# Gathering rows of x itself for the first 7.5 of 49 iterations, with the normalised copy of x made in 14 chunks beside them

## The reference

```python
def _layernorm(x, axis=-1, eps=1e-05):
    m = jnp.mean(x, axis=axis, keepdims=True)
    v = jnp.var(x, axis=axis, keepdims=True)
    return (x - m) / jnp.sqrt(v + eps)
...
        def _gcn_layer(x, W, b, edge_weight, edge_src, edge_dst):
            support = x @ W
            msgs = support[edge_src] * edge_weight[:, None]
            agg = jax.ops.segment_sum(msgs, edge_dst, num_segments=N_NODES)
            return agg + b
        h = jax.nn.elu(_gcn_layer(x, W1, b1, edge_weight, edge_src, edge_dst))
        h = jax.nn.elu(_gcn_layer(h, W2, b2, edge_weight, edge_src, edge_dst))
        return h
...
    x = x + _L0_gnn_ref(_layernorm(x, axis=-1), L0_gnn_W1, L0_gnn_b1, L0_gnn_W2, L0_gnn_b2, edge_weight, src, dst)
    x = x + _L0_ffn_ref(_layernorm(x, axis=-1)[None], L0_ffn_W1, L0_ffn_b1, L0_ffn_Wg, L0_ffn_bg, L0_ffn_Wd, L0_ffn_bd)[0]
```

## Time and profile before

| | us |
|---|---|
| median of three runs | 4646.21 |
| the profiled execution | 4650.56 |
| its span, from first to last instruction | 4648.6 |
| first gather of layer one begins | 87.92 |
| last gather of layer one begins | 2057.25 |
| first gather of layer two begins | 2075.61 |
| busy: TensorE, VectorE, ScalarE, GpSimd | 3573.3, 1952.0, 1053.3, 3235.2 |

### The profile page before, as it was taken

One profiled execution on the slowest core, in us unless ns is written; L12 is line 12 of the kernel. 1 busy time (PEld: TensorE's weight loads), 2 busy tenths in 40 slices (PEclk: granted clock), 3 DMA queues, 4 the chain that ended last, 5 costly groups with the idle time before them and its releaser, 6 DMA issues.

```text
span 4648.6 us, 84335 instructions
## 1 busy us (share of the span) xinstructions
PE 3573.3 (77%) x21450; PEld 3350.1 (72%) x21451; DVE 1952.0 (42%) x6618; ACT 1053.3 (23%) x1720; POOL 3235.2 (70%) x3389
## 2 busy tenths in 40 slices
PE   2776766767767767768888888878788888869998
PEld 1666666666666666658888877878787887758887
DVE  8433333333333333334554454444444444463333
ACT  4100000000000000004333333333333333241111
POOL 5777777777777777767777777777777777604444
PEclk6766666666566666668988888898988888789999
DMA  8333333333333333334544444444444444435554
GB/s 281 113 113 111 113 112 112 112 111 112 112 112 111 112 112 112 113 96 122 148 146 143 145 142 146 143 146 140 146 144 145 146 142 145 122 129 175 179 178 148
DMA packets 248132, 626.46 MB, mean 135 GB/s; under 512 B 63398, under 2 KB 110459, under 8 KB 247491
## 3 DMA queue, kind: packets, MB, share of 16 engines
q0 software_dynamic: 170688, 492.87, 37.2%
q1 hardware_dynamic: 76930, 129.30, 7.8%
HBM read 519.25 MB, written 103.63 MB: 134 GB/s over the span
## 4 chain that ended last, share of the span: by engine, by line
POOL 56%; issue 19%; PE 17%; DMA 4%; DVE 2%; POOLq 1%; ACT 1%; DVEq 0%; SPq 0%; ACTq 0%
POOL rows L542 56%; PE pA L1325 8%; PE pA L1193 4%; DMA rows<-xn_scratch,idx 2%; DMA rows<-h_scratch,idx 1%; PE pB L1234 1%; PE pC L1315 1%; PE pB L1315 1%; PE pC L1216 1%; POOLq L328 1%; PE pT L1303 1%; DMA xn_scratch<-rows 0%; DMA rows<-in_x_dram 0%; DVE stats L754 0%; ACT aggT L696 0%
## 5 line engine op out<-in xcount | busy, mean ns | idle before, releaser
L1193 PE MATMUL pA<-S,rows 128*128 128x96 f32 x12544 | 2140.2, 344 | 957.7 <-DMA rows<-xn_scratch,idx 524.4
L1193 PEld LDWEIGHTS pA<-S,rows 128*128 128x128 f32 x12544 | 2020.3, 254 | 1087.7 <-DMA rows<-xn_scratch,idx 400.5
L542 POOL DMA_INDIRECT rows<-h_scratch,idx x1568 | 1496.0, 954 | 495.0 <-issue 486.2
L542 POOL DMA_INDIRECT rows<-xn_scratch,idx x1568 | 1492.7, 952 | 484.3 <-issue 479.1
L866 DVE TENSOR_SCALAR S<-iota_p,tdst,twgt 128x96 f32<-128x96 f32 x3168 | 875.7, 349 | 9.2 <-issue 8.9
L915 DVE TENSOR_TENSOR aggT<-aggT,pA 128x192 f32 x784 | 274.2, 350 | 1252.6 <-PE pA L1193 1116.0
L924 DVE TENSOR_TENSOR zb<-pZ,brow 128x256 f32<-128x256 f32 x198 | 84.1, 425 | 860.8 <-issue 625.7
L625 ACT ACTIVATE stage<-aggT 128x256 f32 x196 | 81.7, 417 | 1390.2 <-DVE aggT L915 1372.6
L1234 PE MATMUL pB<-work,w 128*128 128x128 f32 x3232 | 386.6, 278 | 0.0
L1325 PE MATMUL pA<-aggT,work 128*128 x1680 | 382.0, 381 | 0.0
L1234 PEld LDWEIGHTS pB<-work,w 128*128 128x128 f32 x3232 | 370.1, 192 | 0.0
(11 more groups left out here) (178 smaller groups left out, 2226.5 us busy)
## 6 DMA issues: line engine op xcount, KB each, us to landing
pay_scratch<-work SPq DMA_DIRECT2D x98, 512.0 KB
rows<-xn_scratch,idx POOLq DMA_INDIRECT x1568, 2.8
rows<-h_scratch,idx POOLq DMA_INDIRECT x1568
h_scratch<-work SPq DMA_DIRECT2D x98, 128.0 KB
pay_scratch<-work SPq DMA_DIRECT2D x98, 128.0 KB
work<-in_x_dram SPq DMA_DIRECT2D x97, 128.0 KB
rows<-in_x_dram SPq DMA_DIRECT2D x24, 512.0 KB, 5.7
xn_scratch<-rows SPq DMA_DIRECT2D x24, 512.0 KB, 6.3
```

The costliest lines, as they stand in the source:

```text
L542: pool.indirect_dma_start(rows[:, s, t, :], None, source, bass.IndirectOffsetOnAxis(at, 0))\
L1193: last = mm(to[:, k * W:(k + 1) * W], rows[:, slot, t, k * P:(k + 1) * P], Sx[:, t, :], start=(t == 0), stop=(t == T - 1))
```

## The change

- The stage-1 pass over x is gone. The sync queue loads only the tables, `src` and `dst` first. VectorE clears one half of `aggT` at the very start, ScalarE the other half behind its table copies; `tsrc` is transposed first, and `stage_idx`, which makes the gathers' indices, stands right behind it.
- Of layer one the halves 0 to 14 gather from `x` itself; the halves from 15 on gather from `xn_d`, and the first of these waits until all 14 chunks of `xn_d` are stored.
- The rows of the halves 0 to 14 are normalised in their slots: `row_statistics` and `row_scales` on VectorE and `row_root` and `row_normalise` on ScalarE, for two groups (a pair) at a time, one half ahead of the half whose products are added. TensorE waits for them (`s_na`) instead of the gathers.
- In each of the halves 0 to 13 one chunk of 896 rows of x is loaded, normalised and stored, with ScalarE's own DMA queue; the functions are `chunk_statistics`, `chunk_scales`, `chunk_root`, `chunk_normalise`, `chunk_store`, `load_chunk`.
- The small tiles for statistics lie in the space of `LG`, the chunks in `work`; both are used for something else only in layer two.

The core of the diff (the lines with # name the engine):

```diff
+    LNT = 7
+    LNR = LNT * P
+    LNC = NB // LNT
+    RAWI = LNC // 2
...
# sync queue
-                             frm[0:BODY * GE].rearrange("(c p e) -> p c e", p=P, e=GE)).then_inc(s_rows, 16)
-                sp.dma_start(to[0:FULL_ROWS - BODY, GCH - 1, :],
-                             frm[BODY * GE:FULL_ROWS * GE].rearrange("(p e) -> p e", e=GE)).then_inc(s_rows, 16)
-                sp.dma_start(to[FULL_ROWS - BODY:FULL_ROWS - BODY + 1, GCH - 1, 0:LAST_EDGES],
-                             frm[FULL_ROWS * GE:E].rearrange("(a e) -> a e", a=1)).then_inc(s_rows, 16)
-            for c in range(4, XAHEAD):
-                sp.dma_start(rows[:, c, :, :], x_chunk(c)).then_inc(s_xin[c], 16)
-            for i in runs(sp, LNI):
...
# GpSimd
+                for par in range(2):
+                    iteration(0, x, 2 * q + par, par)
+            iteration(0, x, RAWI - 1, (RAWI - 1) % 2)
+            gathers(0, x, RAWI, RAWI % 2, 0)
+            pool.wait_ge(s_xst, 16 * LNC + 1)
+            gathers(0, xn_d, RAWI, RAWI % 2, 1)
+            with pool.Fori((RAWI + 1) // 2, ITERS // 2) as q:
+                for par in range(2):
+                    iteration(0, xn_d, 2 * q + par, par)
+            iteration(0, xn_d, ITERS - 1, (ITERS - 1) % 2)
...
# ScalarE
+            def load_chunk(c, buf):
+                act.dma_start(xc[buf], x[chunk_rows(c), :].rearrange("(p t) f -> p t f", t=LNT)).then_inc(s_xin, 16)
+
+            def row_root(pair, s):
+                act.wait_ge(s_var, pair + 1)
+                act.activation(std[:, s:s + 2, :], mv[:, s:s + 2, :, 1], ACT.Sqrt, bias=epsc[:, :]).then_inc(s_std, 1)
+
+            def row_normalise(pair, s):
+                act.wait_ge(s_nmr, pair + 1)
+                for n in range(2):
+                    for t in range(T):
+                        last = act.activation(rows[:, s + n, t, :], rows[:, s + n, t, :], ACT.Identity,
+                                              bias=nmr[:, s + n, t:t + 1], scale=rstd[:, s + n, t:t + 1])
+                    last.then_inc(s_na, 1)
+
...
+                act.wait_ge(s_xnmr, c + 1)
+                for t in range(LNT):
+                    last = act.activation(xc[buf][:, t, :], xc[buf][:, t, :], ACT.Identity,
+                                          bias=xnmr[:, t:t + 1], scale=xrstd[:, t:t + 1])
+                last.then_inc(s_xna, 1)
+
+            def chunk_store(c, buf):
+                hold(act, s_xna, c + 1)
+                hold(act, s_xst, 16 * c + 1)
+                act.dma_start(xn_d[chunk_rows(c), :].rearrange("(p t) f -> p t f", t=LNT), xc[buf])\
+                   .then_inc(s_xst, 16)
...
+            load_chunk(0, 0)
+            act.sem_inc(s_xst, 1)
+            for pair in range(HALF // 2):
+                row_root(pair, 2 * pair)
...
+            with act.Fori(0, RAWI) as i:
+                for half in range(2):
+                    h = 2 * i + half
+                    _, start, end = half_flags(act, h)
+                    ticks(act, start, end, lambda j: tick1(j, h))
+                    ahead = (1 - half) * HALF
+                    row_root(2 * h + 2, ahead)
+                    row_normalise(2 * h + 2, ahead)
+                    chunk_root(h)
+                    row_root(2 * h + 3, ahead + 2)
+                    row_normalise(2 * h + 3, ahead + 2)
+                    chunk_normalise(h, half)
+                    chunk_store(h, half)
+                    load_chunk(h + 1, 1 - half)
+
+            act.wait_ge(s_xin, 16 * (LNC + 1))
             act.preload_act_table(ACT.Exp)
...
# VectorE
+                to = idx[:, bass.ds(at, 1), :, :].rearrange("p a g t -> p (a g) t")
+                v.tensor_copy(to, tsrc[:, :, bass.ds(h * HALF, HALF)].rearrange("p t g -> p g t"))\
+                 .then_inc(s_idx[layer], 1)
...
+                    tc.then(v.tensor_reduce(LO[0:n, c], rdst[0:n, c, :], axis=AX.X, op=ALU.min))
+                dve.wait_ge(s_tcopied, GCH)
+                dve.wait_ge(s_tbl_clear, 3)
+                for at in range(AHEAD):
+                    stage_idx(0, at, at)
                 for c in range(GCH):
                     n = P if c < GCH - 1 else TAILG
                     v.tensor_scalar(rrel[0:n, c, :], rdst[0:n, c, :], LO[0:n, c:c + 1], None, ALU.subtract)\
...
+            tables()
+            dve.wait_ge(s_const, 4)
+            v.tensor_copy(identg[:, :, 0:P], ident[:, :].unsqueeze(1).to_broadcast([P, KH, P])).then_inc(s_const, 1)
...
+            def row_statistics(pair, s, value):
+
+                for n in range(2):
+                    dve.wait_ge(s_gath[0][s + n], value)
+                    for t in range(T):
+                        last = v.bn_stats(stats[:, s + n, t, :], rows[:, s + n, t, :])
+                last.then_inc(s_st, 1)
+                hold(dve, s_st, pair + 1)
+                for n in range(2):
+                    for t in range(T):
+                        last = v.bn_aggr(mv[:, s + n, t, :], stats[:, s + n, t, :])
+                last.then_inc(s_var, 1)
+
...
+
+                dve.wait_ge(s_std, pair + 1)
+                v.reciprocal(rstd[:, s:s + 2, :], std[:, s:s + 2, :]).then_inc(s_rstd, 1)
+                dve.wait_ge(s_rstd, pair + 1)
+                v.scalar_tensor_tensor(out=nmr[:, s:s + 2, :], in0=mv[:, s:s + 2, :, 0], scalar=-1.0,
+                                       in1=rstd[:, s:s + 2, :], op0=ALU.mult, op1=ALU.mult).then_inc(s_nmr, 1)
...
+            def chunk_statistics(c, buf):
+
+                dve.wait_ge(s_xin, 16 * (c + 1))
...
+                if layer == 0:
+                    for pair in range(HALF // 2):
+                        row_statistics(pair, 2 * pair, 16 * T)
+                    for pair in range(HALF // 2):
+                        row_scales(pair, 2 * pair)
+                    with dve.Fori(0, RAWI) as i:
+                        for half in range(2):
+                            h = 2 * i + half
+                            ahead, value = (1 - half) * HALF, (i + half + 1) * (16 * T)
+                            ovf, start, end = half_flags(dve, h)
+                            with dve.If(ovf > 0):
+                                wide_groups(0, h)
+                            row_statistics(2 * h + 2, ahead, value)
+                            ticks(dve, start, end, tick1)
+                            edges_pair(0, h, 0)
+                            row_scales(2 * h + 2, ahead)
+                            chunk_statistics(h, half)
+                            row_statistics(2 * h + 3, ahead + 2, value)
+                            edges_pair(0, h, 2)
+                            chunk_scales(h)
+                            row_scales(2 * h + 3, ahead + 2)
+                            stage_idx(0, h + AHEAD, (i & 1) * 2 + half)
+                with dve.Fori(0 if layer else RAWI, ITERS) as i:
                     for half in range(2):
                         h = 2 * i + half
...
# TensorE
+            def rows_ready(layer, i, h, u, half, raw):
+
+                if raw:
+                    pe.wait_ge(s_na, HALF * h + u + 1)
+                else:
+                    pe.wait_ge(s_gath[layer][half * HALF + u], 16 * T * (i + 1))
+
...
+            with pe.Fori(0, RAWI) as i:
+                for half in range(2):
+                    half_of(0, i, half, True, tick1)
+            pe.wait_ge(s_na, HALF * (LNC + 1))
+            for layer, tick in ((0, tick1), (1, tick2)):
```

More of the change, by code:

```diff
@@ L236, in bass_gnn_then_routed_ffn @@
         s_rows_clear = sem("edge_rows_padded")
[L237 removed]
+        s_rows = [sem(f"edge_rows_loaded_{n}") for n in ("src", "dst", "weight")]
         s_w = sem("weights_loaded")
@@ new lines, in gathers @@
+            def gathers(layer, source, i, par, half):
+                for u in range(HALF):
+                    s = half * HALF + u
+                    if u == 0:
+                        hold(pool, s_idx[layer], 2 * i + half + 1)
+                    hold(pool, s_mm[layer], SLOTS * i + s + 1)
+                    for t in range(T):
+                        at = idx[:, 2 * par + half, u, t:t + 1]
+                        pool.indirect_dma_start(rows[:, s, t, :], None, source,
+                                                bass.IndirectOffsetOnAxis(at, 0))\
+                            .then_inc(s_gath[layer][s], 16)
@@ new lines, in iteration @@
+            def iteration(layer, source, i, par):
+                for half in range(2):
+                    gathers(layer, source, i, par, half)
+            with pool.Fori(0, RAWI // 2) as q:
+                for par in range(2):
[7 more added lines that the diff above has]
+                    iteration(0, xn_d, 2 * q + par, par)
@@ L769, in _ @@
-            for i in runs(dve, LNI):
-                if isinstance(i, int) and i == 1:
-                    tables()
-                first_chunk = isinstance(i, int) and i == 0
-                lnc.base, lnc.n = 0 if first_chunk else 2 * SLOTS * i - 1, 0
-                for s in range(SLOTS):
```

(19 more changed lines are left out.)

322 lines of the change are left out of this document (138 added, 184 removed).

## The result

| | before | after |
|---|---|---|
| median, us | 4645.78 (4644.03 to 4648.02, 6 runs) | 4730.0 (4727.4 to 4733.65, 6 runs) |
| ratio | | 1.0181, 95% interval 1.0168 to 1.0194 |
| profiled execution, its span | 4650.56, 4648.6 | 4729.28, 4727.6 |
| first gather of layer one | 87.92 | 23.88 |
| first gather of half 15 | 390.60 | 476.62 |

The change makes the kernel 84 us slower, 1.8%. The first four experiments were timed where the kernel before took 4656.69 us; all later ones where it took about 5700 us, so each ratio is against the kernel before in its own session. Bare times are therefore 11 us too long in the first four when they are set beside 4730, and of the later ones the text uses ratios and traces rather than times.

What follows compares the result with a forecast made beforehand. GpSimd's gathers, 20.1 us a half, were taken to bound layer one. Half 15 would begin at 476.5 instead of 389.3 us, 87 later: 4738 us profiled, 4733 against the median, which lies 4.4 lower; range 4650 to 4790.

Steps and rivals of the forecast that it cites:

- the ring: In halves 1 to 13 ScalarE (12.9 us) and VectorE (15.4) wait for each other in turn: period 28.3 us.
- Start: Layer one's gathers begin near 18.3 us, 69.6 us earlier, after VectorE's clearing, the casts and the transposes.
- D(0): Moment when VectorE has made the last scales of half 0: 75 us, bounds 68 and 82.
- ScalarE's gap: In each half, ScalarE's completion, waits and two DMA issues 1.0 us, register load and branches 1.4.
- ScalarE's jump back: ScalarE's loop jump in every second half: 0 to 4.1 us for each of six, 12 us taken in all.
- The second tick: Two halves have two ticks; the second waits for TensorE's product, then stage, zneg, zexp: 2.9 us each, 5.8 together.
- 13 turns: From half 0's last scales to half 13's: 13 x 28.3 + 5.8 + 12 us, ending at 460.7.
- The hand-over: Half 15's gathers wait for the last chunk's normalisation, issue and store (7.0), and GpSimd 0.3: 15.8 us.
- The shift: Half 15's first gather moves from 389.3 to 476.5 us, 87 later; nothing differs from there, so the total moves alike.
- Table switches: ScalarE's two tables alternate each half; load taken as 1.28 us without drain; by the skill page 18 us more, 4751.
- first two rivals: GpSimd still paces layer one, 4601 us, chance 0.07; VectorE paces and ScalarE is never late, 4633 or 4659 us, chance 0.11.
- The shorter and the longer ring: Period 24.5 to 27 us, 4670 to 4705, chance 0.14; period above 31 us, 4770 to 4800, chance 0.10.

Runs made afterwards that it cites:

- first four experiments: Kernel after with chunk normalisation and store a half later; VectorE's tick behind the first pair's adds; both; no chunk copy: 4694.6, 4713.86, 4703.85, 4607.77 us.
- e1: Kernel after, with each chunk's normalisation and store moved to the next half, behind that half's first pair: 4694.6 us, ratio 1.0082.
- e6: Kernel after, with VectorE's loop over halves 0 to 13 written out so that it never jumps back: ratio 1.0095.
- e4: Kernel after, with no chunk loaded, normalised or stored; layer one gathers x throughout, rows from half 15 on unnormalised: 4607.77 us, ratio 0.9892.
- e3: e1 plus VectorE's tick placed behind the first pair's adds instead of ahead of them: 4703.85 us, ratio 1.0101.
- e9: e8 with GpSimd instead of VectorE clearing a half of aggT at the start: ratio 1.0024.
- e10: e9 with GpSimd's clearing of aggT cut into ten pieces of 1264 columns: ratio 1.0007.
- e8b: Second run of the e8 kernel: ratio 1.0020.
- e7: e1 and e6 together, run twice: ratios 1.0007 and 1.0027.
- e8: e7 with VectorE's tick behind the first pair's adds and ScalarE's first-pair root ahead of its tick, run twice: ratios 0.9933 and 1.0020.

## Why the prediction was right

The forecast was 4733 us, the median is 4730.0; the mechanism is the one it named: e1 shows that the order costs the time, e6 that VectorE's jump does not, and e4 that the copy is what closes the ring. That the sum came within 3 us is in part luck, since errors cancel:

- **Start.** First gather 18.3 predicted, 23.88 measured. VectorE's clearing began at 3.66, not at 0.9, 2.7 us later, and the transposes of `tsrc` are 32 matmuls in 6.70 us, where I had set the 16 in 4.0 of the earlier trace rows: 2.7 more. GpSimd lost nothing by it: half 2's first gather waits 0.68 us instead of 2. D(0) was due at 75 and came at 80.6: `regs` was ready at 44.5 instead of 39.9, on the late clearing and the slower tables, and the adds of half 0 began 6 us late, behind a wait for the first product that the prediction did not have:

```profile
67.30 0.35 DVE L920 TENSOR_TENSOR aggT<-aggT,pA 128x192 f32 x1 [3.18 <-PE pA L1266]
```

- **The ring.** 12.9 + 15.4 = 28.3 predicted; 13.7 + 15.2 = 28.9 measured.
- **ScalarE's gap.** For completion, DMA issues, registers and branches I had 2.4 us, taken in part from VectorE's gap ahead of a tick; it was 3.7 to 4.0.
- **ScalarE's jump back.** 12 us for six jumps, the middle of 0 and 25; measured 0, since turns with and without it are the same (28.7 to 28.9 and 28.9 to 29.2). This is the term that was most wrong. In its place stood the 0.6 us by which the ring is longer, 8 us in 13 turns, and 2.4 us more for the two second ticks.
- **The second tick.** 2.9 us predicted, 33.0 - 28.9 = 4.1 measured. The table load stands in the tick's own loop and is done again, with no other table loaded in between:

```profile
120.94 1.28 ACT L606 ACT_TABLE_LOAD   x1 [3.79 <-issue]
...
125.08 1.28 ACT L606 ACT_TABLE_LOAD   x1 [1.36 <-PE pZ L1276]
```

- **13 turns.** Predicted 368 + 5.8 + 12 = 385.7, measured 464.31 - 80.42 = 383.9.
- **The hand-over.** 15.8 us predicted, 12.3 measured (464.3 to 476.62). The store's issue is at 472.30, 8.0 us behind the scales, where I had 8.5, and GpSimd goes 4.3 us later, where I had 7.3; the 7.0 for the store came from the 6.3 of the earlier trace rows, measured on busier queues.

```profile
472.30 0.35 ACTq L686 DMA_DIRECT2D xn_scratch<-work  x1
```

- **The shift.** 87 us at half 15 predicted, 86.0 measured; from the right row, 390.60, the prediction's own 476.5 would have given 85.9. The end moved only 79.0 (spans 4648.6 and 4727.6): the step "from there on nothing differs" failed by 7 us. 5.5 of them come back in layer one itself, where the 1328 gathers from half 15 take 1661.2 us from the first start to the last, instead of 1666.7 (947 ns for one instead of 951). Why they are shorter, nothing here shows.
- **From trace to median.** The profiled execution was forecast at 4738 us and took 4729.28, 9 too many. The 4.4 us that were then subtracted, because the profiled execution before lay that far above its median, had no counterpart after: 4729.28 lies 0.7 below the median of 4730.0. This cancels over half of the miss, by luck.
- **Table switches.** The rows after show what the earlier trace rows showed: an activation ends at 305.01, the load starts at 305.02, takes 1.28, the next activation starts at 306.32. No drain stands there, so the 18 us which the figure of the Trainium skill ("ScalarE: Activation LUTs", "What ACT_TABLE_LOAD costs") would have added did not come.

```profile
304.61 0.40 ACT L623 ACTIVATE aggT<-zeros 128x256 f32 x1
...
305.02 1.28 ACT L662 ACT_TABLE_LOAD   x1
...
306.32 0.30 ACT L662 ACTIVATE LG<-LG,epsc 128x8 f32<-128x8 f32 x1
```

The first two rivals fell on the row they were tied to: L975 waits 3.7 to 8.3 us in the halves with one tick instead of 1, so neither GpSimd nor VectorE paces. The shorter and the longer ring fell on the period, 29.5 us in the mean. The break-even of the first, a mean period of 23.0 us, lies between e4, at a mean of 20.9 and faster than before, and e1, at 26.4 and slower; e4 has no hand-over, so this is no close test.

## What to carry to other kernels

Before work is moved beside a stage in which some engine idles, write down for each pair of engines what each does between the other's result and its own next one. If both lists are closed, the period is their sum, however idle the engines are. What opened the ring here was to put the new work behind the result that the other waits for (e1: 42 us for the same work in another place). Then look for what the opened ring leaves: here the table load and the root, and a loop's jump back, both hidden before.

## What the runs showed of the hardware

- ScalarE's register load, branches and DMA issue show as 0.2 us of idle time while its activations still run (e1), and as 3.74 us behind a wait for its own last result, with one DMA issue more (the kernel after).
- VectorE's jump back to the start of a long loop body takes 5.3 to 5.8 us ahead of the statistics where 1.3 stand without it, and 8.3 to 10.2 in e1 and e3, where 896 KB are loaded at that moment. There the 1.3 us grow too, to 1.6 to 2.2, and in e4, which loads no chunk, the jump takes 5.3 to 6.4. That the load is the cause is argued from this, not shown by a run that moves the load alone.

```profile
354.78 2.71 DVE L929 BATCH_NORM_STATS2 LG<-rows 128x6 f32<-128x256 f32 x8 [5.84 <-issue]
```

- GpSimd's clearing of SBUF keeps a VectorE cast out for the rest of its length, 6.5 us here and 6.8 in pieces. The Trainium skill, "SBUF — State Buffer", section "SBUF: two separate sides", says that the pair of ports which the two share goes, against a VectorE instruction in a two-port mode, to whichever starts first, for that whole instruction, and that the other is blocked meanwhile. e9's row agrees with the blocking; whether the cast runs in such a mode no run here shows. e10's, where the cast stands through the ends of six pieces, goes beyond it.
- 32 matmuls of a table's transpose took 6.70 us at 15.5 us and 3.99 at 30.6 us. The granted clock was 1.00, the level of 2.4 GHz, in both stretches, as the windows show; the cause is open.

```profile
15.52 6.70 PE L1233 MATMUL pB<-flip,aggT 128*128 128x128 f32 x32 [15.52 <-DVE aggT L774]
...
30.57 3.99 PE L1233 MATMUL pB<-flip,aggT 128*128 128x128 f32 x32
```
```profile
14.00:23.00 9.00, 6.70 (x32) 6.41 (x32) 5.60 (x13) 1.99 (x4) 0.00 (x0) 1.00 0.09 7
30.00:35.00 5.00, 4.55 (x41) 4.05 (x38) 4.08 (x8) 2.08 (x5) 3.78 (x5) 1.00 0.71 118
```

- In the later sessions every version that ran there, the kernel before too, took about 5700 us, some 1050 more. The instructions that were compared are as long as elsewhere (four `S` 1.04 us, eight normalisations 4.04); between them engines stand without a releaser, or for one that the profile calls remote, as TensorE here in layer two of e8b:

```profile
2503.45 0.32 PE L1278 MATMUL pA<-S,rows 128*128 128x96 f32 x1 [2.48 <-issue]
```

The cause is unknown, and it leaves one question open: whether e7 or e8 beats the kernel before where that takes 4646 us.
